# The second layer's choice of blocks: a 0 or 1 product on GpSimd in place of a pass in each up product, and the down pieces taken over two banks

## The reference, cut to what matters

```python
    xf = x.reshape(-1, IN_F)
    prob = jax.nn.softmax(xf @ router_w.T + router_b, axis=-1)
    _, idx = jax.lax.top_k(prob, TOPK)                 # TOPK = 4 of NBLK = 16
    mask = jnp.zeros((n, NBLK), bool).at[jnp.arange(n)[:, None], idx].set(True)
    h = jnp.einsum('nd,ibd->nib', xf, w1b) + b1b       # 16 blocks of 64
    h = jnp.where(mask[:, :, None], h, jnp.zeros((), h.dtype))
    h = jax.nn.relu(h)
    y = jnp.einsum('nib,dib->nd', jnp.where(mask[:, :, None], h, 0.0), w2b) + b2
```

## Time and profile before

| | us |
|---|---|
| median of 3 runs | 1379.82 (1377.99 to 1381.21) |
| the profiled execution, its own time | 1376.99 |
| its span, first to last instruction | 1375.3 |
| busy PE, PEld in the span | 1321.1, 1109.3 |
| busy DVE, ACT, POOL in the span | 1058.0, 937.5, 194.6 |

### The profile page before, as it was taken

The page is one execution under the profiler, slowest core; times in us unless marked ns, Lnnn a source line. Parts: engine busy times, 40 slices in busy tenths (PEclk is TensorE's granted clock), DMA queues, the critical chain, the costliest instruction groups (busy, mean ns, idle before and its releaser), DMA issues.

```text
span 1375.3 us, 29939 instructions
## 1 busy us (share of the span) xinstructions
PE 1321.1 (96%) x10448; PEld 1109.3 (81%) x10448; DVE 1058.0 (77%) x3292; ACT 937.5 (68%) x2357; POOL 194.6 (14%) x564
## 2 busy tenths in 40 slices
PE   4789999999999999999999999999999799999998
PEld 2577888878888887888888888878887588999897
DVE  6968996998799699969996996999699665544542
ACT  5769885887689588858886885888588533333333
POOL 4612111111111111111110111111111200000000
PEclk8999999999999999999999999999999999999999
DMA  6552232323233232313232332324131221111100
GB/s 212 191 160 86 93 115 71 102 101 106 66 107 102 84 88 78 130 58 115 101 105 68 103 105 73 100 73 135 52 120 67 79 69 43 43 43 43 43 16 31
DMA packets 88327, 123.02 MB, mean 89 GB/s; under 512 B 8577, under 2 KB 74482, under 8 KB 88178
## 3 DMA queue, kind: packets, MB, share of 16 engines
q1 hardware_dynamic: 87858, 121.11, 27.6%
q10 hardware_dynamic: 320, 0.00, 0.0%
HBM read 101.69 MB, written 19.40 MB: 88 GB/s over the span
## 4 chain that ended last, share of the span: by engine, by line
PE 77%; ACT 12%; DVE 4%; issue 2%; DMA 0%; POOL 0%; SPq 0%; DVEq 0%; ACTq 0%; POOLq 0%
PE at L848 15%; PE at L861 10%; PE at L900 9%; PE at L927 8%; PE at L1580 7%; PE at L971 7%; PE at L1616 7%; ACT prob L1113 5%; PE at L938 2%; PE at L881 2%; PE at L892 2%; PE at L886 1%; ACT probT L1122 1%; ACT area_raw L1070 1%; PE at L955 1%
## 5 line engine op out<-in xcount | busy, mean ns | idle before, releaser
L1113 ACT ACTIVATE prob<-prob,low 128x512 f32<-128x512 f32 (+3 forms) x512 | 280.8, 551 | 115.8 <-DVE low L1267 115.8
L1267 DVE CUSTOM_DVE_ANT_0 prob<-at,mask 128x512 f32<-128x512 f32 (+3 forms) x512 | 219.8, 486 | 8.8 <-PE at L861 8.8
L848 PE MATMUL at<-w_hi,c_lo 128*128 128x386 f32 x512 | 189.4, 370 | 1.5 <-DVE area_raw L1212 1.5
L848 PE MATMUL at<-w_hi,c_hi 128*128 128x386 f32 x512 | 173.7, 339 | 0.0
L848 PE MATMUL at<-w_lo,c_hi 128*128 128x386 f32 x512 | 173.6, 339 | 0.0
L1280 DVE TENSOR_SCALAR prob<-prob,rec 128x512 f32<-128x512 f32 (+3 forms) x512 | 169.6, 395 | 4.5
L900 PE MATMUL at<-ident,prob 128*128 128x128 f32 x1280 | 165.6, 276 | 3.1 <-DVE low L1267 1.7
L927 PE MATMUL at<-probT,v 128*64 128x512 f32 (+3 forms) x1024 | 151.9, 438 | 4.4 <-DVE probT L1290 2.8
L900 PEld LDWEIGHTS at<-ident,prob 128*128 128x128 f32 x1280 | 143.5, 142 | 10.6 <-DVE yT_lo L1296 1.6
L927 PEld LDWEIGHTS at<-probT,v 128*64 128x64 f32 x1024 | 75.5, 136 | 83.8 <-issue 69.1
L1122 ACT ACTIVATE probT<-at 128x512 f32<-128x512 f32 (+1 forms) x256 | 130.2, 536 | 5.4 <-PE at L900 2.7
(11 more groups left out here) (225 smaller groups left out, 3221.9 us busy)
## 6 DMA issues: line engine op xcount, KB each, us to landing
area_w<-in_L_ffn_w SPq DMA_DIRECT2D x65, 1024.0 KB, 5.7
bias<-in_L_ffn_w SPq DMA_DIRECT2D x160, 32.0 KB, 4.6
x_in<-in_L_attn_x SPq DMA_DIRECT2D x8, 512.0 KB, 5.4
xr<-in_L_attn_x SPq DMA_DIRECT2D x8, 512.0 KB, 5.0
eo_d<-hidT SPq DMA_DIRECT2D x32, 128.0 KB, 1.8
x_d<-xr SPq DMA_DIRECT2D x8, 512.0 KB, 3.0
area_raw<-x_d SPq DMA_DIRECT2D x8, 512.0 KB, 4.0
out<-area_raw SPq DMA_DIRECT2D x8, 512.0 KB, 2.9
```

The lines of the kernel that those rows point to most:

```text
L848: m = eng.matmul(bQ[n % 2][:, 0:W], a[:, (j // HP) % 2, k, n * P:(n + 1) * P], w[:, k, j % HP, :], start=start, stop=(k == KC - 1 and a is ...
L1113: eng.activation(sl, sl, ACT.Exp, scale=-1.0, bias=low[:, i:i + 1], accum_out=den[:, i:i + 1]).then_inc(exp_done.sem, 1)
L1267: eng.tensor_tensor_reduce(out=prob[s % 2][h][:, off[c]:off[c + 1]], in0=bC[i][:, at:at + (c + 1) * P], in1=mask[:, (NT - 1 - c) * P:T], s ...
```

## The change

Where a block isn't chosen, the hidden units are no longer shut by a pass on TensorE in front of the relu, but multiplied by 0 after it, on GpSimd.

- The flags stay 0 or 1 (`opens`; the last tensor_scalar of `choose` is gone). TensorE transposes them (`turn_open`), VectorE copies them to `openT`, and SyncE (`get_open`) stores them in DRAM (`open_d`, 32 KB) and, when that has landed, loads them back with four DMAs, each row to 64 partitions: `is_open` is [128, 8, 512] fp32, 2 MB in all. The first two DMAs bring chunks 0 to 3, the others 4 to 7.
- An up product has 6 passes. A bank is free when the one fp32 relu is done. `spread`, `sp` and their preparation are gone.
- GpSimd (`keep`) multiplies `hT` of each chunk by `is_open`, in place, [128, 512] fp32.
- ScalarE makes `hT_hi` from the kept `hT` in SBUF (`high`), four chunks later than the relu; the last four come at the end of the turn.
- TensorE's down takes pieces 0 and 2 together, chunk by chunk, in two banks; then `turn_open`, then piece 1, then piece 3.

```diff
+        def get_open(b):
+            eng.wait_ge(openT_done.sem, openT_done.at(b))
+            eng.dma_start(open_d[b], openT[0:NB, :]).then_inc(open_store.sem, open_store.unit)
+            eng.wait_ge(open_store.sem, open_store.at(b))
+            eng.wait_ge(kept_done.sem, kept_done.at(b - 1))
+            eng.wait_ge(g["outputs_made"].sem, g["outputs_made"].at(B - 1))
+            rows = open_d[b].rearrange("(h two) t -> two h t", two=2)
+            for i in range(2):
+                hs = slice(i * HC // 2, (i + 1) * HC // 2)
+                for j in range(2):
+                    eng.dma_start(is_open[j * P // 2:(j + 1) * P // 2, hs, :], rows[j, hs, :].partition_broadcast(P // 2)).then_inc(
+                        open_load[i].sem, open_load[i].unit)
+        get_open(0)
         for b in range(0, B - 2):
             free(eng, b + 1)
             get_x(eng, b + 2)
             get_eo(eng, b + 2)
+            get_open(b + 1)
             put(b)
+        get_open(B - 1)
...
         def up(b, hs):
             for h in hs:
                 if h == 0:
-                    eng.wait_ge(relu_done.sem, relu_done.at(b - 1, HC - 1))
+                    eng.wait_ge(relu32_done.sem, relu32_done.at(b - 1, HC - 1))
...
-                eng.matmul(bU[h % 2][:, :], spread[:, h, :], shutT[:, b % 2, :], start=True, stop=False)
-                product(b, bU[h % 2], up_hi[:, :, h, :], up_lo[:, :, h, :], False, pe_up)
+                product(b, bU[h % 2], up_hi[:, :, h, :], up_lo[:, :, h, :], pe_up)
 
         def down(b, ns):
+            o = {n: bD[n // 2][:, (n % 2) * C:(n % 2 + 1) * C] for n in ns}
             for n in ns:
...
-                o = bD[n // 2][:, (n % 2) * C:(n % 2 + 1) * C]
-                eng.matmul(o, mem[:, n * P:(n + 1) * P], backT[:, :], start=True, stop=False)
-                for h in range(HC):
-                    if n == 0:
-                        eng.wait_ge(relu_done.sem, relu_done.at(b, h + 1))
-                        eng.wait_ge(relu_lo_done.sem, relu_lo_done.at(b, h + 1))
+                eng.matmul(o[n], mem[:, n * P:(n + 1) * P], backT[:, :], start=True, stop=False)
+            for h in range(HC):
+                if ns[0] == 0:
+                    eng.wait_ge(relu_done.sem, relu_done.at(b, h + 1))
+                    eng.wait_ge(relu_lo_done.sem, relu_lo_done.at(b, h + 1))
+                for n in ns:
                     for part, w in ((hT_lo, downT_hi), (hT_hi, downT_lo), (hT_hi, downT_hi)):
...
         def turn(b):
...
-            down(b, (0, 1))
-            turn_shut(b + 1)
-            down(b, (2, 3))
+            down(b, (0, 2))
+            turn_open(b + 1)
+            down(b, (1,))
+            down(b, (3,))
...
-        def relu(b, hs):
-            for h in hs:
-                eng.wait_ge(pe_up.sem, pe_up.at(b, h + 1))
-                eng.wait_ge(relu_lo_done.sem, relu_lo_done.at(b - 1, h + 1))
-                eng.activation(hT[:, h, :], bU[h % 2][:, :], ACT.Relu, bias=b1[:, h:h + 1]).then_inc(relu32_done.sem, relu32_done.unit)
-                eng.activation(hT_hi[:, h, :], bU[h % 2][:, :], ACT.Relu, bias=b1[:, h:h + 1]).then_inc(relu_done.sem, relu_done.unit)
+        def relu(b, h):
+            eng.wait_ge(pe_up.sem, pe_up.at(b, h + 1))
+            eng.wait_ge(relu_lo_done.sem, relu_lo_done.at(b - 1, h + 1))
+            eng.activation(hT[:, h, :], bU[h % 2][:, :], ACT.Relu, bias=b1[:, h:h + 1]).then_inc(relu32_done.sem, relu32_done.unit)
+
+        def high(b, h):
+            eng.wait_ge(kept_done.sem, kept_done.at(b, h + 1))
+            eng.activation(hT_hi[:, h, :], hT[:, h, :], ACT.Copy).then_inc(relu_done.sem, relu_done.unit)
 
         def turn(b):
             memory(b)
-            relu(b, range(0, 3))
-            copy_x(b + 1)
-            relu(b, range(3, HC))
...
+            for h in range(HC):
+                if h == 3 and b + 1 < B:
+                    copy_x(b + 1)
+                if h >= 4:
+                    high(b, h - 4)
+                relu(b, h)
+            for h in range(HC - 4, HC):
+                high(b, h)
...
+        def keep(b, h):
+            eng.wait_ge(relu32_done.sem, relu32_done.at(b, h + 1))
+            eng.wait_ge(open_load[2 * h // HC].sem, open_load[2 * h // HC].at(b))
+            eng.tensor_tensor(hT[:, h, :], hT[:, h, :], is_open[:, h, :], ALU.mult).then_inc(kept_done.sem, kept_done.unit)
+        power(0)
+        for b in range(B):
+            if b + 1 < B:
+                power(b + 1)
+            for h in range(HC):
+                keep(b, h)
```

More of the change, by code:

```diff
@@ L1479, in second_layer @@
     hT = g["hT"]
-    hT_hi, hT_lo, mem = (g["hidden"][k] for k in ("hT_hi", "hT_lo", "mem"))
+    hT_hi, hT_lo, mem, is_open = (g["hidden"][k] for k in ("hT_hi", "hT_lo", "mem", "open"))
     area = g["area_sq"]
@@ L1566, in router, with turn_open, product @@
             m.then_inc(pe_r.sem, pe_r.unit)
-        def turn_shut(b):
-            eng.wait_ge(shut_done.sem, shut_done.at(b))
+        def turn_open(b):
+            eng.wait_ge(open_done.sem, open_done.at(b))
             for n in range(NT):
-                m = eng.transpose(bF[0][0:NB, n * P:(n + 1) * P], shut[:, n, :], ident[:, :])
-            m.then_inc(pe_shut.sem, pe_shut.unit)
-        def product(b, bank, hi, lo, first, done):
-            start = first
+                m = eng.transpose(bF[0][0:NB, n * P:(n + 1) * P], opens[:, n, :], ident[:, :])
+            m.then_inc(pe_open.sem, pe_open.unit)
+        def product(b, bank, hi, lo, done):
+            start = True
             for k in range(KC):
@@ L1586, in memory @@
             eng.wait_ge(lo_done.sem, lo_done.at(b))
[L1587 removed]
             eng.wait_ge(mem_done.sem, mem_done.at(b - 1))
[L1589 removed]
+            product(b, bMem, readT_hi, readT_lo, pe_mem)
         def up(b, hs):
@@ L1628, in first @@
             output(3)
-            turn_shut(0)
+            turn_open(0)
             eng.wait_ge(prepared.sem, prepared.at(0))
@@ L1646, in last @@
             up(b, range(HC))
-            down(b, range(NT))
+            down(b, (0, 2))
+            down(b, (1,))
+            down(b, (3,))
         first()
@@ L1693, in gpsimd, with power @@
         eng.wait_ge(mem_one.sem, mem_one.at(0))
-        for b in range(0, B):
+        def power(b):
             eng.wait_ge(var_done.sem, var_done.at(b))
@@ L1786, in front @@
             output(3)
-            copy_shut(b)
+            copy_open(b)
         def turn(b):
@@ L1795, in turn @@
             relu_low(b, range(6, HC))
-            copy_shut(b + 1)
+            copy_open(b + 1)
             finish(b)
```

81 lines of the change are left out of this document (31 added, 50 removed).

## The result

The changed kernel is slower by far more than forecast: 1414.91 us, the median of 4 runs (1414.52 to 1421.04), against 1380.35 for the kernel before (median of 4). The ratio is 1.0252, its 95% interval 1.0228 to 1.0277. The sign of the prediction is right; its size (1383, range 1371 to 1393) is not. The profiled execution took 1415.08, with a span 37.8 us longer than in the earlier trace rows.

The account below looks back on a forecast made before the run. TensorE was taken to bound each 32.24 us turn; shorter ups and pairing gave 30.3, a down stall 32.85. 7 x (32.85 - 32.24) + 1.0 - 1.95 = +3.3 us, a predicted median of 1383, range 1371 to 1393.

Parts of the forecast that it names:

- the walk: Offset-by-offset schedule of one second-layer turn across the engines, giving 32.85 us, 0.6 more than before.
- Products 0 to 2 run 5.8 to 9.5: GpSimd's first three products of a turn, at these offsets in us, each put at 1.18 us.
- rival 3: Flags land late, so GpSimd's products wait; at 6 us per 512 KB, +38 us, 1418; chance 0.04.
- The exclusion itself: GpSimd's product and VectorE operations with two SBUF operands, or split's cast, never run together; the one waiting longer goes next.
- Rival 1: Exclusion weak or VectorE goes first, only the order costs: turns of 31.35, 1371.6 us; chance 0.28.
- The stall in down: TensorE waits 2.55 us a turn before chunk 6 in the down pair, for VectorE's lo 6.
- The product: GpSimd's 128x512 multiply put at 1.18 us, bounds 1.09 and 1.41; each 0.1 moves a turn by 0.5.
- The order alone: Without exclusion, choose standing between lo 5 and lo 6 leaves 1.05 us of stall in down.
- The removed pass: One of seven TensorE passes per up goes, 0.23 us each: 1.84 a turn, 14.8 us for 64 ups.
- The pair of pieces: Taking two down pieces together saves a change between fp32 and fp32r passes: 0.1 us a turn, bounds 0 to 0.3.
- The flags' way: Store and reload through DRAM land in time, at most 0.4 us a turn; the first turn costs 1.0 more.
- The last turn: Without copy_x, router, split or choose, hi 7 comes before down needs it: gains 1.95 us.

Follow-up runs that it names:

- experiment 6: Changed kernel with turn_x after up 4 instead of up 2 and copy_x after relu 4; norm and products still collide: 1395.18 us.
- experiment 1: Changed kernel with GpSimd's product cut from 512 to 8 columns of each chunk, all waits and transfers kept: 1372.33 us.
- experiment 3: Changed kernel with GpSimd's first product of a turn waiting until VectorE's norm of the next sequence is done: 1394.06 us.
- experiment 7: Changed kernel with the product moved to VectorE, which reads bank and flags in one instruction, its list written anew: 1371.60 us, ratio 0.9944 to the kernel before.
- experiment 4: Kernel before without the seventh pass of each up and nothing in its place, the choice of blocks left out: 1374.72 us.
- experiment 8: Kernel before, its pass kept, with only the down pieces reordered to 0 and 2 together, then 1, then 3: 1379.86 us.
- experiment 10: Changed kernel with the down pieces one by one (0, 1, turn_open, 2, 3) instead of 0 and 2 as a pair: 1443.35 us.
- experiment 2: Changed kernel with the flags loaded once, for the first sequence, and used for all eight, the small store kept: 1412.72 us.

## Why the prediction was wrong

By turn 1's rows the turn grew by 37.67 - 32.24 = 5.43 us. TensorE's busy time at full clock is 30.75 (experiment 6, the same work), 1.49 less than before; the low clock adds 32.59 - 30.75 = 1.84; the waits are 37.67 - 32.59 = 5.08, of them 2.66 before turn_x and 2.38 in down. The prediction had 0.6 for a turn.

- **The step that failed** is in the walk, "Products 0 to 2 run 5.8 to 9.5", with turn_x following up 2 without a wait. The products' start was right (offset 5.7, as against 5.8). But norm's four tensor_scalars run at just that offset, and I had left them out of the list of what a product excludes: it named operations with two SBUF operands and the cast, and these have one operand in SBUF and two scalars per partition. They take 1345 ns, not 408, beside a product (experiments 1 and 3 give 408 and 409 without one). The stall is 2.66, where the walk had none. None of the four rivals had it either: rival 3's 1418 is near the measured time by chance. Nor did the walk ask what norm's end holds up, though turn_x is the one thing in the first half of a turn on which TensorE waits for VectorE. The Trainium skill, SBUF — State Buffer, section on SBUF's two separate sides, counts among the lock's holders a VectorE operation "in a 2-port perf mode", not only one with two inputs. The Trainium skill, VectorE: DVE Perf Modes, on the tier table, gives fp32 tensor_scalar between SBUF operands twice the plain rate, which would put it in such a mode. The trace agrees with the blocking. It can't tell the rate of norm's steps, which come at 256 columns only: 408 ns, beside 390 on average for a tensor_scalar of the first layer of the same size with one scalar per partition, whose time grows from 288 at 128 columns to 485 at 512.
- **A term that was missing**: the sum has none for the clock. In turn 1 the idle 2.66 us was followed by 4.14 at a clock of 0.59, 1.84 us lost. With both waits in a turn the clock fell seven times in six turns, four times behind the wait before turn_x and three times behind the one in down. With the wait before turn_x shortened to 1.0 (experiment 6) or gone (experiment 3) it fell in two turns of six, each time in down, at the same price (1.57 and 1.60).
- **The exclusion itself** was right. Where a product and a low are both wanted they alternate, lows go from 0.69 to 1.28 on average and choose falls between lo 5 and lo 6, as walked. Rival 1 is refuted.
- **The stall in down** was put at 2.55 a turn before chunk 6. It is 2.38, in two parts, 0.37 before chunk 4 and 2.01 before chunk 6, both for VectorE's lo. The size is right, in part by luck: the walk had no wait before chunk 4. Since norm was late everything behind it was too, so the two numbers don't stand for the same walk: experiment 3, with norm mended, has 2.77 there.
- **The product** was put at 1.18 us; undisturbed it is 1.27 to 1.29. By the prediction's own slope (0.5 us a turn for 0.1) that is some 0.5 a turn, inside the bounds. The estimate of 1.11 from the Trainium skill, GPSIMD Engine Reference, section on performance versus the Vector engine, is further off than the line through the rows.
- **The order alone** was put at 1.05 of stall and a turn of 31.35. With short products the turn is 31.21 (experiment 1), but its parts are 0.62 of stall and 30.59 of work where 30.3 was expected, and a product of 0.24 us isn't one of 1.18. The total is near, the terms are not.
- **The removed pass** was put at 1.84 with nothing else in the way, and a full 1.89 shows in experiment 7 (32.24 to 30.35). The one read of a bank that comes with it I had valued at 0; without it 1.35 is all (experiment 4). **The pair of pieces** was put at 0.1 and is 0 alone (experiment 8), while in the changed kernel it spares 3.4 (experiment 10); the walk used it without pricing it.
- **The flags' way.** GpSimd waited for them once, 5.1 us in the first turn; rival 3 is out. The first turn was put at 1.0 above the others and came 0.8 below them (36.87), as the late flags let norm go first.
- **The last turn** was to gain 1.95. The last two came to 68.05; with 37.67 for the one before the last 30.38 is left, where before 63.88 - 32.22 = 31.66 was: 1.3 gained. With short products it is 60.89 - 31.22 = 29.67, 2.0 gained.
- **The sum.** Turn by turn the differences to before are 4.6, 5.4, 5.5, 5.5, 7.1, 5.4, and 4.2 for the last two: 37.8 in all, the 37.8 of the span, where the prediction had +3.3. Of a usual turn's 5.4 it had 0.6; nearly all of the rest is the stall before turn_x (2.66) and the clock (1.84). Turn 4 is 1.6 longer than the others in TensorE's busy time (34.19), which is the clock's price once more.

## What to carry to other kernels

When work is moved to GpSimd, list every VectorE operation between SBUF operands that can meet it, one-input forms too, and ask for each who waits for it; the sum of idle time on both engines says nothing. A stall of TensorE may cost its length and then nearly 2 us more in clock, so the waits of such a turn, 5.1 us, are to be counted as 6.9. And if VectorE would be held for about as long as it would need to do the work itself (0.75 us with the bias from PSUM, beside 1.28 on GpSimd), let it do it.

## What the runs showed of the hardware that I had not expected

- A GpSimd tensor_tensor of [128, 512] fp32 holds off a VectorE tensor_scalar of [128, 256] with one SBUF tensor and two scalars per partition: 1345 ns beside it, 408 alone. Only the product's length and place were varied, not the operands of VectorE's operation, so which of its reads makes it wait is open. GpSimd is held as well: a product that began 0.11 us after VectorE's tensor_tensor of 1024 columns took 2.28 us.
- The granted clock fell after 2.66 us without any matmul (0.59 mean over the next 4.14 us), but not each time: behind that wait it fell in four turns of six in the changed kernel and in three of six without the reload (experiment 2), and in the others behind the wait in down. It fell in two turns of six after waits of 0.89 and 1.86 us with 2.4 us of work between (experiment 3). After a wait of 1.0 us before turn_x it never fell (experiment 6, six turns). After 1.96 us in down it fell in two of those six, and in turns 4, 5 and 6 of the changed kernel. What decides is open.
- Transfers of 2 MB a turn ran at up to 377 GB/s beside VectorE and GpSimd without lengthening their operations by more than some 2% (without them, in experiment 2, products average 1541 ns against 1575, lows 1262 against 1281, norm's steps 1017 in both). The flags themselves are slow to land: 512 KB, four issued together, took 8.2 us from issue in the median.
- The start of the second layer differs by up to 8 us between kernels that are the same up to there but for the small preparation of `spread` (1100.6 to 1108.8), in single profiled executions. Turns are the finer measure for a change in that layer.
